# Both attentions of a two-layer model on one core: scores by row groups, the maximum inside the exponential, v in two masked copies, and a new order of the steps

## What is computed

```python
x = x + conv0(ln(x))     # 8 heads of 16, softmax over 7 neighbours of a token, bias by position
t = t + ffn0(ln(t))      # GELU experts, 2 shared and 8 routed
x = x + conv1(ln(x))     # full softmax attention in a window of 64, with mask and biases
t = t + ffn1(ln(t))      # spline experts, the best 2 of 8
```

## Time and profile before

| | |
|---|---|
| three runs | 1105.59, 1101.36, 1099.24 us; median 1101.36 |
| the profiled execution | 1100.1 us, its span on the core 1098.5 us |
| first attention | 10.1 to 113.3 us |
| GELU experts | to about 430 us |
| second attention | 432.6 to 533.5 us |
| routing | to about 600 us |
| spline experts | to the end |
| TensorE busy over the span | 984.8 us (90%) |
| VectorE, ScalarE, GpSimd busy | 716.5, 560.5, 446.4 us (65, 51, 41%) |

### The profile page before, as it was taken

How to read it: one execution, slowest core, us unless ns; L and a number is a source line. 1 busy time by engine, 2 the same in 40 slices (tenths; PEclk the granted TensorE clock), 3 DMA queues, 4 the chain that set the end, 5 groups by cost and what they waited for, 6 DMA issues and landing times. The chain is left out here.

```text
span 1098.5 us, 22480 instructions
## 1 busy us (share of the span) xinstructions
PE 984.8 (90%) x7705; PEld 906.8 (83%) x7705; DVE 716.5 (65%) x1496; ACT 560.5 (51%) x1121; POOL 446.4 (41%) x338
## 2 busy tenths in 40 slices
PE   5887599988959997988798999999999999999993
PEld 5676489887949996866544999999999999999993
...
GB/s 70 1 0 1 128 222 206 363 165 229 225 234 348 149 129 15 1 0 1 82 0 173 144 150 260 97 184 95 98 138 170 128 208 95 134 126 31 9 6 8
DMA packets 24942, 132.55 MB, mean 121 GB/s; under 512 B 3114, under 2 KB 14644, under 8 KB 17732
## 3 DMA queue, kind: packets, MB, share of 16 engines
...
## 5 line engine op out<-in xcount | busy, mean ns | idle before, releaser
L1294 PE MATMUL kan_ps_h<-kan_xf,kan_w 128*128 128x128 f32 x2496 | 304.3, 275 | 0.6 <-DMA kan_w<-w_dram 0.6
L1294 PEld LDWEIGHTS kan_ps_h<-kan_xf,kan_w 128*128 128x128 f32 x2496 | 291.2, 192 | 1.4 <-DMA kan_w<-w_dram 1.4
L727 ACT ACTIVATE f_hid<-f_ps_up,f_wt 128x512 f32<-128x512 f32 x160 | 108.3, 689 | 160.8 <-PE f_ps_up L676 160.6
L1308 PE MATMUL kan_ps_y<-kan_w,kan_hf 128*128 128x128 f32 x1248 | 154.9, 278 | 8.3 <-DVE kan_hf L1446 8.3
L1517 POOL DMA_INDIRECT out<-kan_y_sb,kan_slots_y x39 | 64.3, 1648 | 233.9 <-ACT kan_y_sb L1392 233.9
L1308 PEld LDWEIGHTS kan_ps_y<-kan_w,kan_hf 128*128 128x128 f32 x1248 | 148.2, 195 | 8.8 <-issue 8.8
L676 PE MATMUL f_ps_up<-f_n_part,f_w_part 128*128 128x512 f32 x480 | 128.4, 422 | 28.7 <-DVE f_w_part L756 22.6
L687 PEld LDWEIGHTS f_ps_dn<-f_wt,f_hid 128*128 128x128 f32 x1280 | 148.3, 192 | 2.8
L687 PE MATMUL f_ps_dn<-f_wt,f_hid 128*128 128x128 f32 x1280 | 148.6, 275 | 0.0
L797 DVE SCALAR_TENSOR_TENSOR x_sb<-f_ps_dn,f_mix_now,x_sb 128x128 f32<-128x128 f32 x160 | 44.7, 344 | 154.1 <-PE f_ps_dn L687 154.1
L676 PEld LDWEIGHTS f_ps_up<-f_n_part,f_w_part 128*128 128x128 f32 x480 | 95.3, 205 | 48.9 <-issue 28.5
...
## 6 DMA issues: line engine op xcount, KB each, us to landing
...
```

What stands on the lines that cost most here:

```text
L727: eng.activation(hid[s % 2][:, c, :], ps_up[c][:, :], ACT.Gelu, bias=wt[a][:, 2 * FF0 + c:2 * FF0 + c + 1]).then_inc(acted.sem, 1)
L1294: mm = eng.matmul(ps_h[n % 2][:, m, :], w12[n % 2][:, at:at + P], rhs, start=(c == 0), stop=(c == BASES))
L1308: mm = eng.matmul(ps_y[n % 2][:, :], lhs, w3[n % 2][:, i * P:(i + 1) * P], start=(i == 0), stop=(i == CH1 * FEAT - 1))
```

## The change

Six things change, all in `attention` and in what is loaded for the second one:

- **Scores.** q is spread only over two masked copies (even heads, odd heads of each pair), by two scaled activations on ScalarE; GpSimd's `spread_heads` is gone. Each score matmul uses the 32 rows of one pair of heads (a row group of the array) and 128x64 columns. Eight of them go over four row groups, each pair into a PSUM bank of its own. The scores have one PSUM tile of four banks instead of two of one.
- **Softmax.** `shift` is gone. VectorE's maximum is written negated, and ScalarE takes eight exponentials, one a head, with it as their bias.
- **v.** It lies in two masked copies, written by ScalarE as two strided copies into buffers that GpSimd clears at the start. `mix` makes 16 matmuls of 64 columns instead of 8 of 128, two accumulate, and the result needs no mask. VectorE reads it in one instruction, in the second attention with the bias of v added.
- **PSUM.** The turned x and the output share banks with z. So `turn_x` waits for z of five tiles before, and `mix` for the output sum of the tile before and for a copy of x.
- **Order.** The step orders are new, and the steps are written out for all tiles, without a loop; waits are on constants.
- **Loads.** The two bias rows of the second attention become a row for the output and a column of 128 single numbers for v: three transfers instead of two.

The diff, cut to its core; functions that it takes out stand above in the kernel:

```diff
--- before.py
+++ after.py
@@ -163,13 +163,8 @@
-    LAG = 4
-    V_BUFFERS = LAG
+    V_BUFFERS = 4
     ident = consts[:, C_ID:C_ID + P]
-    head_scales = consts[:, C_HEAD:C_HEAD + HEADS]
-    half_of = [consts[:, C_HALF + i:C_HALF + i + 1] for i in range(2)]
     bq, bk, bv, bp = w.get("bq"), w.get("bk"), w.get("bv"), w.get("bp")
     with ExitStack() as own:
...
         moments, rstd, stats_vector, stats_scalar = layer_norm_stats(sb, sem, "ln", x_sb, eps, x_stats, x_arrivals)
         xn = two("xn", [P, P])
         xnT = two("xnT", [P, P])
-        qT = two("qT", [P, P])
         kT = two("kT", [P, P])
-        v = [sb(f"v{i}", [P, P]) for i in range(V_BUFFERS)]
-        q_heads = two("q_heads", [P, 2, HEADS, BLK])
+        v = [sb(f"v{i}", [P, 2, P]) for i in range(V_BUFFERS)]
+        q_heads = two("q_heads", [P, 2, 2, BLK])
         logits = two("logits", [P, HEADS, keys])
         probs = two("probs", [P, HEADS, keys])
         weights = two("weights", [P, HEADS, BLK])
         probsT = two("probsT", [P, PAIRS, P])
-        top = two("top", [P, HEADS])
+        below = two("below", [P, HEADS])
         total = two("total", [P, HEADS])
         zT = two("zT", [P, P])
-        ps_x = ps("ps_x", [P, P])
-        ps_out = ps("ps_out", [P, 1, P])
+        q_scale = sb("q_scale", [P, 2])
+        q_bias = sb("q_bias", [P, 2])
+        ps_S = ps("ps_S", [P, PAIRS, GROUP, P])
+        ps_Z = ps("ps_Z", [P, 2, GROUP, P])
+        ps_P = ps("ps_P", [P, PAIRS, P])
         ps_qkv = ps("ps_qkv", [P, 3, P])
...
+        ps_x = ps_Z[:, 1, 1, :]
+        ps_out = ps_Z[:, 0, 1, :]
...
+        MIX = 5
+        LAST = 7
         def stage(work):
-            def run(turn, n):
-                if not isinstance(turn, int) or 0 <= LAG * turn + n < TILES:
-                    work(turn, n)
+            def run(n):
+                if 0 <= n < TILES:
+                    work(n)
             return run
-        def tile(turn, n):
-            return bass.ds(LAG * turn + n, 1)
+        def after(eng, count, n):
+            if n >= 0:
+                eng.wait_ge(count, n + 1)
...
+                def turn_x(n):
+                    after(eng, normed, n)
+                    after(eng, z_ok, n - MIX)
+                    eng.transpose(ps_x, xn[n % 2][:, :], ident).then_inc(turned, 1)
+                def project(n):
+                    after(eng, xnT_ok, n)
+                    for c in (q_ok, k_ok, v_ok):
+                        after(eng, c, n - 1)
...
+                def score(n):
+                    after(eng, q_ok, n)
+                    after(eng, k_ok, n)
+                    after(eng, biased, n - 1)
+                    for b in range(2):
+                        for hp in range(PAIRS):
+                            rows = slice(2 * DK * hp, 2 * DK * (hp + 1))
+                            mm = eng.matmul(ps_S[:, hp, 0, b * BLK:(b + 1) * BLK],
+                                            q_heads[n % 2][rows, b, :, :],
+                                            kT[n % 2][rows, b * BLK:(b + 1) * BLK], start=True, stop=True)
+                    mm.then_inc(scored, 1)
+                def turn_probs(n):
+                    after(eng, norm_p, n)
+                    after(eng, probsT_ok, n - 1)
                     for hp in range(PAIRS):
                         mm = eng.transpose(ps_P[:, hp, :], weights[n % 2][:, 2 * hp:2 * hp + 2, :], ident)
...
+                    mm.then_inc(probs_turned, 1)
+                def mix(n):
+                    after(eng, probsT_ok, n)
+                    after(eng, v_ok, n)
+                    after(eng, added, n - 1)
+                    after(eng, xnT_ok, min(n + MIX - 1, TILES - 1))
                     eng.sem_inc(gate, 1)
                     for hp in range(PAIRS):
                         cols = slice(2 * DK * hp, 2 * DK * (hp + 1))
                         for b in range(2):
                             rows = slice(b * BLK, (b + 1) * BLK)
...
+                            for r in range(2):
+                                mm = eng.matmul(ps_Z[cols, b, 0, 0:BLK], v[n % V_BUFFERS][rows, r, cols],
+                                                probsT[n % 2][rows, hp, r * BLK:(r + 1) * BLK],
+                                                start=(r == 0), stop=(r == 1))
+                    mm.then_inc(mixed, 1)
+                def project_out(n):
+                    after(eng, z_ok, n)
+                    eng.matmul(ps_out, zT[n % 2][:, :], w["wo"], start=True, stop=True).then_inc(out_done, 1)
+                for i in range(TILES + LAST):
+                    score(i - 2)
+                    project(i - 1)
+                    mix(i - MIX)
+                    turn_probs(i - 4)
+                    turn_x(i)
+                    project_out(i - MIX)
             @block.scalar
             def _(eng):
...
+                eng.wait_ge(q_ready, 1)
+                def copy_x(n):
+                    after(eng, turned, n)
+                    after(eng, proj, n - 2)
+                    eng.activation(xnT[n % 2][:, :], ps_x, ACT.Copy).then_inc(xnT_ok, 1)
+                def scale_q(n):
+                    after(eng, proj, n)
+                    after(eng, scored, n - 2)
+                    for r in range(2):
+                        q = ps_qkv[:, 0, :].rearrange("p (b i) -> p b i", b=2)
+                        if bq is not None:
+                            ins = eng.activation(q_heads[n % 2][:, :, r, :], q, ACT.Identity, scale=q_scale[:, r:r + 1],
+                                                 bias=q_bias[:, r:r + 1])
+                        else:
+                            ins = eng.activation(q_heads[n % 2][:, :, r, :], q, ACT.Copy, scale=q_scale[:, r:r + 1])
+                    ins.then_inc(q_ok, 1)
+                def copy_k(n):
+                    after(eng, proj, n)
+                    after(eng, scored, n - 2)
+                    if bk is not None:
+                        eng.activation(kT[n % 2][:, :], ps_qkv[:, 1, :], ACT.Identity, bias=bk).then_inc(k_ok, 1)
                     else:
...
+                        eng.activation(kT[n % 2][:, :], ps_qkv[:, 1, :], ACT.Copy).then_inc(k_ok, 1)
+                def copy_v(n):
+                    if n == 0:
+                        eng.wait_ge(zeroed, V_BUFFERS)
+                    after(eng, proj, n)
+                    after(eng, mixed, n - V_BUFFERS)
+                    for r in range(2):
+                        heads = "p (h r c) -> p h r c"
+                        ins = eng.activation(v[n % V_BUFFERS][:, r, :].rearrange(heads, r=2, c=DK)[:, :, r, :],
+                                             ps_qkv[:, 2, :].rearrange(heads, r=2, c=DK)[:, :, r, :], ACT.Copy)
+                    ins.then_inc(v_ok, 1)
+                def exponentials(n):
+                    after(eng, topped, n)
+                    after(eng, norm_p, n - 2)
+                    for h in range(HEADS):
+                        ins = eng.activation(probs[n % 2][:, h, :], logits[n % 2][:, h, :], ACT.Exp,
+                                             bias=below[n % 2][:, h:h + 1])
+                    ins.then_inc(exped, 1)
+                def copy_probs(n):
+                    after(eng, probs_turned, n)
+                    after(eng, mixed, n - 2)
+                    eng.activation(probsT[n % 2][:, :, :], ps_P[:, :, :], ACT.Copy).then_inc(probsT_ok, 1)
+                for i in range(TILES + LAST):
+                    copy_k(i - 2)
+                    scale_q(i - 2)
+                    copy_v(i - 2)
+                    copy_x(i - 1)
+                    copy_probs(i - 5)
+                    exponentials(i - 3)
             @block.gpsimd
             def _(eng):
...
+                for b in range(V_BUFFERS):
+                    eng.memset(v[b][:, :, :], 0.0).then_inc(zeroed, 1)
                 arrived(eng)
...
+                def normalise(n):
+                    after(eng, inv, n)
+                    after(eng, probs_turned, n - 2)
...
+                for i in range(TILES + LAST):
                     if bp is not None:
-                        add_bp(turn, n)
-                steps(eng, step)
+                        add_bp(i)
+                    normalise(i - 5)
             @block.vector
             def _(eng):
...
+                half = consts[:, C_HALF:C_HALF + 2]
+                if bq is not None:
+                    eng.tensor_scalar(q_bias[:, :], half, bq, DK ** -0.5, ALU.mult, ALU.mult)
+                eng.tensor_scalar(q_scale[:, :], half, DK ** -0.5, None, ALU.mult).then_inc(q_ready, 1)
...
+                def add_bias(n):
+                    after(eng, scored, n)
+                    after(eng, exped, n - 2)
+                    eng.tensor_tensor(logits[n % 2][:, :, 0:BLK].rearrange("p (h b) k -> p h b k", b=2),
+                                      ps_S[:, :, 0, :].rearrange("p h (b k) -> p h b k", b=2),
```

(46 more changed lines are left out.)

252 lines of the change are left out of this document (40 added, 212 removed).

## The result

The changed kernel takes 1079.6 us in the median of four runs (1066.51 to 1094.56), where the kernel before takes 1100.3. That the median meets the forecast 1079 is therefore luck.

What follows compares the result with a forecast made beforehand. VectorE was taken to set the attentions' pace, 5.6 us of work in a 5.55 us interval. Savings of 11.9 and 9.7 less 0.7 for the transfer make 20.9, so 1100.1 becomes 1079 us, range 1069 to 1092.

Steps and rivals of the forecast that it cites:

- What sets the pace: Attention tiles: a cycle through exponentials, VectorE's sums, z, turning of x and ScalarE's copies, 4.99 us at full clock.
- I take 5.1 and 5.05: Interval from tile to tile in the first and second attention, where it was 5.55 and 5.40 us.
- TensorE's own 5.4 is longer than the cycle: Attention tiles at half clock: TensorE's work of 5.4 us a tile exceeds the cycle of 5.1.
- my sum had 3.7: TensorE's work in the attentions at full clock: 3.7 us a tile.
- third to a half at the lower level: Share of attention steps expected with TensorE at half clock, behind the intervals of 5.1 and 5.05 us.
- Rival 1: Half clock throughout both attentions: steps of 5.4 us, 9.8 us more, 1089 us; chance 0.18.
- The fills: First normalisation to first exponential: 7.8 us in the first attention, saving 3.8; the second saves 3.2.
- The drains: Last exponential to end of last statistics: 0.3 us worse in each attention.
- The transfer: Second attention's third load, bv as 128 single numbers: costs 0.7 us, bounds 0 and 2.6.
- What an attention saves shifts the rest: Whole program: the change touches only the attentions, so later blocks just start earlier by what these save.
- The rule on the clock: TensorE's clock falls only after long idle gaps; set aside, as it would give steps 4.99 and 4.9, about 1074 us.

Runs made afterwards that it cites:

- the profile at the lower level: The changed kernel run once more, nothing altered: 1068.6 us in the median of four, ratio 0.9722; its profiled execution spans 1067.1 us.
- z first: Changed kernel with the GELU block's copy written as a reduction, and z taken ahead of the row sums on VectorE: 1054.7 us, ratio 0.9579.

## Why the prediction was right, and where it was wrong

Two steps of the prediction failed, each by about 5 us: the size of the steps in the attentions, and the premise that the rest of the program stays as it is. Either alone would have left the time at about 1074, inside the range. Together they make 1068.7, the time of the execution that the spans below are from.

- **What sets the pace.** Right: the cycle over eight exponentials, 4.82 us where 4.99 was worked out. Exponentials 0.345 long and 0.244 apart; ScalarE the one waited for; the turning of x right behind z; the score's records within 0.67 (0.8 allowed), the mix's in 0.50 (0.7 taken).
- **The step "I take 5.1 and 5.05" failed.** Measured 4.74 and 4.68 in the mean. Against 5.1, the first attention's five intervals at full clock are 1.4 us shorter in all, the six at half 0.8, and the last two, with less in the cycle, 1.5, which I had counted as full ones. Behind the step stood "TensorE's own 5.4 is longer than the cycle" at half clock. That was wrong: with eight exponentials the steps at half clock are 4.98, and the cycle sets them there too, since the turning follows z by 0.12 us as at full clock (shown above). TensorE's work at half clock is thus at most 4.98 us a tile, and at full clock 3.0, where my sum had 3.7. The "third to a half at the lower level" came true (six of 15) and cost 0.16 us a step. Rival 1, a step of 5.4, doesn't occur.
- **The fills** were right: 7.68 and 8.22 for 7.8 and 8.3.
- **The drains** were worse than forecast: 10.15 and 10.21, not 8.7 and 8.6. Three tiles are mixed after the last exponentials have begun, one and a half and two before the change, and the timeline shows what the new order adds:

```profile
89.27 2.06 ACT L368 ACTIVATE a_probs<-a_logits,a_below 128x70 f32<-128x70 f32 x8 [1.83 <-DVE a_below L438]
...
92.41 1.04 POOL L396 TENSOR_TENSOR a_weights<-a_probs,a_total 128x512 f32<-128x512 f32 x1 [2.85 <-DVE a_total L450]
...
93.89 0.74 PE L298 MATMUL a_ps_Z<-a_probsT,a_v 64*32 64x64 f32 x32 [0.54 <-issue]
94.56 1.11 PE L283 MATMUL a_ps_P<-consts,a_weights 128*128 128x128 f32 x4
```

  The last product ends at 93.45 and its turning starts only at 94.56, since TensorE first mixes the tile before: 1.1 us that my sum had left out.
- **The transfer** of bv was right, taken at 0.7: the first normalisation of the second attention starts 4.4 us after the last statistics of the block before, and 4.3 in the profile at the lower level, where it was 3.5. VectorE's wait for the transfer alone misleads, 1.47 us against 0.24, as it begins earlier. The issue of bv lasts 0.93 here, 0.42 in the profile at the lower level, and the wait is 1.36 there:

```profile
441.83 0.93 SPq L1569 DMA_DIRECT2D bv_col<-in_rows  x1
```

- **"What an attention saves shifts the rest"** was wrong by 5 us at the lower level. From the spans 1098.5 and 1067.1 (the changed kernel again), 31.4 less: attentions 14.4 and 12.1 (11.9 and 9.7 forecast), GELU stretch 1.7, routing and spline experts 4.1, and 1.0 lost ahead of the first attention. Routing and spline experts last 565.0 and 565.5 us in the two profiles with the old attention untouched and 556.6 to 562.7 in all others, so they gain in every kernel with an edited attention, by an amount that varies. A part of it is in the routing block: from the start of the last statistics the gate's products end after 15.3 us before and after 13.1 in the changed kernel. The granted clock over them is 0.50 throughout before; after the change it is 1.00 for some of them. What raised it no run singled out, and the rest of the 4.1 us stays open. At the upper level the untouched GELU block gives 26 us back. I had read none of its rows.
- **The rule on the clock.** I had put the Trainium skill's rule aside ("TensorE: Matmul & The Clock Gate", section "Why this matters for your kernels") since the clock fell with TensorE busy 11.00 of 13.60 us. (By its own steps of 4.99 and 4.9 the time under that rule comes to 1075, not 1074.) The runs don't bear the rule out as the whole story: with waits of 1.80 us and 6.45 of 9.90 busy the clock fell again and again. With waits of 0.46 and 92% busy it stayed at 2.4 GHz for 50 us, and with z first, 13.54 busy of 17.00 and waits up to 1.13 us, it held too. But in that kernel's second attention it fell with no wait above 1.0 us, so neither the longest wait nor the busy share alone orders the cases.
